# Mask maxima split on GpSimd, a shorter log series and a scalar head-norm shift, with all orders laid anew, in a fused attention and Mamba2 kernel

## The chip, the cores and the metric

One core of one Trainium2 chip runs the kernel. The metric is the device time of one execution in microseconds (us), given as the median of several runs. PE is TensorE, DVE is VectorE, ACT is ScalarE, POOL is GpSimd, and SP is SyncE, which here only issues transfers.

## What is computed

64 sequences of 128 tokens with 256 features pass a cross-attention layer with a layer norm, a Mamba2 block and a second cross-attention. Cut to what matters:

```python
q = relu(queries @ Wq + bq); k = relu(keys @ Wk + bk); v = relu(values @ Wv + bv)   # 16 heads of 16
scores = where(row_mask, q_ @ k_ / sqrt(16), 1e-9)
x = layernorm(softmax(scores) @ v_ + queries) * gamma + beta
zxbcdt = rms(x, norm_w) @ in_proj_w                       # z 512, xBC 768, dt 8
dt = softplus(zxbcdt[..., -8:] + dt_bias)
xBC = silu(conv4(xBC) + conv_b)
h = h * exp(dt * A) + (dt * xh) B ; y = h C               # scan over the tokens, state 128
x = x + rms((y + D_skip * xh) * silu(z), gnorm_w) @ out_proj_w
out = x + softmax(ln(x) @ Wq (enc @ Wk)^T / sqrt(32)) @ (enc @ Wv) @ Wo    # 8 heads of 32
```

## The kernel before, in words

Sequences go in 32 groups `g` of two sequences `b` (NB = 2), each with 256 tokens. Every engine has one program: small functions (pieces) such as `q(g, m)` or `scan(g, b)`, and behind them a list of calls that is written out by hand. The list has a head, a loop `for g in range(NG - 9)` of 23 turns, in which pieces of up to six groups interleave (`k(g+7, 0)` of a late group beside `wp(g+2, 0)` of an early one), and a tail. Each engine works through its list in order; semaphores tie the engines together. A wait stands inside the piece that needs it. A turn of the loop is one group's worth of work.

Matrix products go to eight PSUM banks. The table `USES` says which bank each of the 63 uses of a turn takes; `bank()` (line 183) looks up the use before it in the same bank and returns the semaphore that tells it is free. So a new order needs a new table. `unread()` and `warm()` are matmuls whose results nobody reads; they fill places in head and tail.

The pieces the change and the prediction speak of:

- **q, k, v, sA** (PE). Projections as three products of high and low halves (line 332), and the raw scores, for their maxima (line 399). ACT splits the inputs, `split_x` (line 1384) and `split_c` (1395), and evicts, `qe` (1416), `ke` (1427, two or four pieces) and `ve` (1439). POOL forms the low halves, `lo_x` (1842) and `lo_c` (1847), and multiplies the row mask in, `qm` (1861).
- **mA, nm, nw** (DVE). `mA` (line 835) takes the negated maxima of 16 heads, 128x16 numbers for a sequence. `nm` (line 847) casts them to the matmul's type into `NM`, `nw` (line 854) writes the remainder. TensorE transposes `NM` in `tn` (line 412), ACT writes `NT` (line 1449), and the second scores `sT` (lines 432 and 436) use it to subtract the maxima. `eA` (1463) takes the exponential; `av` (456) and `ot` (442) follow, then on DVE `rc` (863), the reciprocal of the sum, `xo`, and the layer norm.
- **cp, dp, bd** (PE). In-projection, the dt columns and a transpose. DVE does the convolution's `tap` (line 991) and `xc` (1004), ACT `ac` and `th`.
- **dc** (DVE, line 940 on). Softplus needs log(1 + u). With r = u / (u + 2) it is 2 r (1 + r^2/3 + r^4/5 + ...) to r^12/13, written as 12 steps on 128x16 numbers; each waits for the one before.
- **scan, lg, yd** (DVE, lines 1015, 1024, 1044). The decay goes out to DRAM and comes back spread over 128 partitions as `DB`, 512 KB for a sequence.
- **hs, hg, hr, hm** . Norm of the second attention. `hm` (DVE, line 1081) computes minus mean times the reciprocal deviation, one number a partition, for ACT's `hx`. `r2` (POOL, 1952) is the power of the RMS norm.
- **tC, sC, oC, q1, k1, v1, wp** (PE). Second attention. `fin` and `store` end a group.

SP issues all loads and stores: `load_x` (line 236, tile xT), `load_c` (243, cT), `load_t` (258, xt), `load_u` (267, cT again for the second attention), `load_m` (280, QM, 128 KB), `dec_out` (286), `dec_in` (294, DB) and `store` (300). All but QM, DB and `dec_out` are 256 KB. A load waits until the tile's last reader is done, and what is behind it waits as well.

Of the kernel before, what the change touches and what calls it, by code (L numbers as in the profile page):

```python
# [2116 lines left out]
```

## Time and profile before

| what | before |
| --- | --- |
| three runs | 1319.29, 1319.77, 1320.99 us, median 1319.77 |
| the profiled execution | span 1319.5 us (its own time is not given beside it) |
| PE busy | 1303.4 us, 99% |
| DVE busy | 1193.6 us, 90% |
| ACT busy | 1131.2 us, 86% |
| POOL busy | 947.7 us, 72% |
| DMA | 87.03 MB, mean 66 GB/s |

The span is from the first to the last instruction of the profiled execution. Busy time is the time in which an engine executed at least one instruction; for PE the ends of matmuls are modelled. The DMA queue q1 carries the kernel's own transfers, q8 and q14 carry instructions to the engines. A share of busy time is a mean over head, loop and tail, which differ.

### The profile page before, as it was taken

The page shows a single profiled execution, that of the slowest core. Times are in us where ns is not written, and L with a number is a line of the kernel's source. Part 1 is how long each engine was busy: PE and PEld are TensorE (multiplying, and loading weights), DVE is VectorE, ACT ScalarE, POOL GpSimd, SP SyncE. Part 2 cuts the span into 40 slices and gives each one's busy share as a digit, 9 for nine tenths or more (in the row PEclk, how much of TensorE's full clock was granted, in tenths as well). Part 3 has the DMA queues.
Part 4 walks back from the last instruction along what each step waited for, and adds up shares of the span by engine and source line. Part 5 has one row for each costly group of instructions (what it writes and reads, how often), then busy time and mean ns, then how long its engine had stood idle before and what let it go on. Part 6 is the DMA issues. An engine that isn't in the chain of part 4 may idle for free.

```text
span 1319.5 us, 43916 instructions
## 1 busy us (share of the span) xinstructions
PE 1303.4 (99%) x15877; PEld 1165.5 (88%) x15877; DVE 1193.6 (90%) x3032; ACT 1131.2 (86%) x3407; POOL 947.7 (72%) x1214
## 2 busy tenths in 40 slices
PE   8999999999999999999999999999999999999998
PEld 7888888999888898888998888899888889898887
DVE  6999999999999999999999999999999999999882
ACT  6778888898888898888898888899888899888866
POOL 4777777777777777777677777687777677677674
PEclk9999999999999999999999999999999999999999
DMA  6121122212122212122211122211122222011210
GB/s 208 48 74 50 50 74 78 78 49 67 50 70 78 78 50 66 50 70 78 78 57 59 50 70 78 78 60 57 50 70 78 77 82 62 17 51 58 66 49 25
DMA packets 41285, 87.03 MB, mean 66 GB/s; under 512 B 5744, under 2 KB 10992, under 8 KB 41072
## 3 DMA queue, kind: packets, MB, share of 16 engines
q1 hardware_dynamic: 40560, 83.93, 20.4%
q8 instruction: 129, 2.11, 0.7%
q14 instruction: 84, 0.69, 0.2%
q10 hardware_dynamic: 512, 0.31, 0.1%
HBM read 75.53 MB, written 8.68 MB: 64 GB/s over the span
## 4 chain that ended last, share of the span: by engine, by line
PE 92%; DVE 4%; POOL 2%; issue 1%; DMA 1%; ACT 1%; DVEq 0%; ACTq 0%; POOLq 0%
PE bank L332 28%; PE bank L442 11%; PE bank L573 7%; PE bank L432 5%; PE bank L399 5%; PE bank L456 5%; PE bank L556 5%; PE bank L587 4%; PE bank L692 4%; PE bank L627 3%; PE bank L380 3%; PE bank L648 3%; PE bank L677 2%; PE bank L490 2%; PE bank L436 1%; PE bank L531 1%
## 5 line engine op out<-in xcount | busy, mean ns | idle before, releaser
L991 DVE SCALAR_TENSOR_TENSOR ACC<-bank,cw,ACC 128x250 f32<-128x250 f32 (+2 forms) x576 | 264.5, 462 | 6.4 <-ACT ACC L1561 3.7
L332 PE MATMUL bank<-xnT,wnl 128*128 128x256 f32 x640 | 198.6, 310 | 1.7 <-DVE XC L1004 1.4
L1648 ACT ACTIVATE PC<-bank,stc 128x128 f32<-128x128 f32 x512 | 182.8, 388 | 8.0 <-DVE stc L1103 5.2
L332 PE MATMUL bank<-xnL,wnh 128*128 128x256 f32 x640 | 178.7, 279 | 0.0
L332 PE MATMUL bank<-xnT,wnh 128*128 128x256 f32 x640 | 178.3, 279 | 0.0
L835 DVE TENSOR_REDUCE sta<-bank 128x4 f32<-128x512 f32 x256 | 163.6, 672 | 2.8 <-PE bank L399 2.8
L1015 DVE TENSOR_TENSOR_SCAN L<-DB,id 128x1024 f32<-128x1024 f32 x64 | 146.6, 2290 | 2.2 <-DMA DB<-dec_scratch 2.2
L1967 POOL TENSOR_TENSOR PC<-PC,stc 128x512 f32<-128x512 f32 x128 | 132.4, 1043 | 11.7 <-DVE stc L1110 11.5
L1463 ACT ACTIVATE PTA<-bank 128x512 f32<-128x512 f32 x256 | 133.5, 629 | 6.8 <-PE bank L436 3.9
L332 PEld LDWEIGHTS bank<-xnT,wnl 128*128 128x128 f32 x640 | 120.4, 188 | 21.4 <-issue 16.2
L1922 POOL TENSOR_TENSOR XH<-XH,dtt 128x512 f32<-128x512 f32 x64 | 81.0, 1265 | 56.6 <-ACT XH L1578 56.6
L332 PEld LDWEIGHTS bank<-xnL,wnh 128*128 128x128 f32 x640 | 120.8, 189 | 0.1
L332 PEld LDWEIGHTS bank<-xnT,wnh 128*128 128x128 f32 x640 | 120.1, 188 | 0.0
L1648 ACT ACTIVATION_READ_ACCUMULATOR PC<-bank,stc 128x1 f32 x512 | 116.7, 228 | 0.0
L1847 POOL TENSOR_TENSOR cL<-cT,cH 128x512 fp32r<-128x512 f32 x31 | 59.0, 1903 | 76.8 <-ACT cH L1395 76.8
L1561 ACT ACTIVATE ACC<-bank,cw 128x256 f32<-128x256 f32 x192 | 110.6, 577 | 2.2 <-PE bank L332 1.5
L1931 POOL TENSOR_TENSOR Y<-Y,SZ 128x512 f32<-128x512 f32 x64 | 85.9, 1342 | 18.8 <-DVE Y L1044 16.1
L1937 POOL TENSOR_TENSOR Yl<-Y,Yh 128x512 fp32r<-128x512 f32 x64 | 82.2, 1285 | 17.4 <-ACT Yh L1606 17.4
L1449 ACT ACTIVATE NT<-bank,sel 128x128 fp32r<-128x128 f32 x256 | 73.6, 382 | 21.5 <-PE bank L412 21.5
L1662 ACT ACTIVATE PTC<-bank 128x512 f32<-128x512 f32 x128 | 78.8, 622 | 15.3 <-PE bank L442 15.2
L1103 DVE TENSOR_REDUCE stc<-bank 128x4 f32<-128x512 f32 x128 | 84.3, 681 | 6.9 <-PE bank L652 6.7
L1569 ACT ACTIVATE bank<-ACC 128x256 f32<-128x256 f32 x192 | 79.6, 418 | 11.1 <-DVE ACC L991 10.8
(210 smaller groups left out, 4757.7 us busy)
## 6 DMA issues: line engine op xcount, KB each, us to landing
DB<-dec_scratch SPq DMA_DIRECT2D x64, 512.0 KB, 4.0
cT<-in_cT SPq DMA_DIRECT2D x64, 256.0 KB, 2.7
xt<-in_xt SPq DMA_DIRECT2D x32, 256.0 KB, 3.7
out_x<-X SPq DMA_DIRECT2D x32, 256.0 KB, 4.0
xT<-in_xT SPq DMA_DIRECT2D x31, 256.0 KB, 4.1
QM<-qm_rows SPq DMA_DIRECT2D x31, 128.0 KB, 4.0
XC<-in_win SPq DMA_DIRECT2D x2, 644.0 KB, 6.8
PTC<-in_wout SPq DMA_DIRECT2D x2, 256.0 KB, 4.6
```

The costliest lines, as they stand in the source:

```text
L332: mm = e.matmul(t[:, c0:c0 + T], wt[:, k, m:m + 128], x[:, k, :], start=(n == 0), stop=(n == 5))
L442: mm = e.transpose(t[:, c0 + i * 128:c0 + (i + 1) * 128], src(i), ident[:, :])
L573: e.matmul(t[:, 0:256], x[:, kk * 128:(kk + 1) * 128], w[:, kk, :], start=(n == 0), stop=(n == 11))
L835: e.tensor_reduce(sta[ns % 4][:, 4 * j:4 * j + 4], t[:, :].rearrange("p (i k) -> p i k", i=4), AX_X, ALU.max, negate=True).then_inc(s_mA, 1)
L991: e.scalar_tensor_tensor(out=w, in0=t[:, 0:T].rearrange("p (b t) -> p b t", b=NB)[:, :, 0:125 + k], scalar=cw[:, c, k:k + 1], in1=w, op0=A ...
L1015: e.tensor_tensor_scan(L[:, :, :].rearrange("p h t -> p (h t)"), DB[b][:, :], id8[:, :, :].rearrange("p h t -> p (h t)"), 0.0, ALU.mult, A ...
L1103: e.tensor_reduce(stc[g % 4][:, 4 * i:4 * i + 4], t[:, :].rearrange("p (i k) -> p i k", i=4), AX_X, ALU.max, negate=True).then_inc(s_mC, 1)
L1463: e.activation(PTA[n % 4][:, :, :], t[:, :].rearrange("p (i k) -> p i k", i=4), ACT.Exp).then_inc(s_eA, 1)
L1561: e.activation(ACC[n % 3][:, :, :], t[:, 0:T].rearrange("p (b t) -> p b t", b=NB), ACT.Identity, bias=cw[:, c, 4:5], scale=cw[:, c, 3:4]). ...
L1648: op = e.activation(PC[n % 4][:, p, :], t[:, p * 128:(p + 1) * 128], ACT.Exp, bias=stc[g % 4][:, 4 * i + p:4 * i + p + 1], accum_out=stc[g ...
L1931: e.tensor_tensor(cv(Y[:, :]), cv(Y[:, :]), SZ[:, :, b * 128:(b + 1) * 128], ALU.mult).then_inc(s_ga, 1)
L1967: e.tensor_tensor(PC[n % 4][:, :, :], PC[n % 4][:, :, :], stc[g % 4][:, 16 + 4 * i:20 + 4 * i].unsqueeze(2).to_broadcast([128, 4, 128]), A ...
```

## The change

1. `nm` and `nw` leave DVE's program and stand in POOL's (lines 1861 and 1868 of the changed kernel), with the same waits.
2. The log series has five fitted coefficients for its seven terms, so `dc` has 10 steps and not 12.
3. `hm` is a `tensor_scalar` with the second factor as a per-partition scalar.
4. SP waits for `d_qr` ahead of the second group of late weights, and DVE's first `xs` for the small parameters.
5. The orders of all five engines and the bank table are new. Each turn has the same 55 pieces on PE, 68 on ACT and 9 on SP; DVE has 88 for 94, POOL 33 for 29. The dummy matmuls keep their counts; only their places shift.

```diff
+ATANH = (1.000000004, 0.33333157341, 0.20012455137, 0.13980301434, 0.14089167199)
 USES = [
-    (("k", 1, 1), 3), (("ot", 0, 2), 5), (("z", 1, 3), 2), (("sT", 4, 2), 1), (("sT", 5, 2), 5), (("sT", 6, 2), 6),
+    (("k", 1, 1), 3), (("ot", 0, 2), 0), (("z", 1, 3), 2), (("sT", 4, 2), 5), (("sT", 5, 2), 0), (("sT", 6, 2), 1),
...
                     if g == 2:
+                        e.wait_ge(d_qr, 16)
...
         def vector(e):
...
-            def nm(g, b):
-                if ok(g):
-                    ns = 2 * g + b
-                    w = sta[ns % 4][:, 0:16].rearrange("p (j i) -> p j i", j=4)
-                    if ns == 0:
-                        e.wait_ge(z_pad, 9)
-                    if ns >= 2:
-                        e.wait_ge(s_tn, ns - 1)
-                    e.wait_ge(s_mA, 4 * ns + 4)
-                    e.tensor_copy(NM[ns % 2][:, :, 0:4], w).then_inc(s_nm, 1)
-
-            def nw(g, b):
...
-                    e.wait_ge(s_nm, ns + 1)
-                    e.tensor_tensor(NM[ns % 2][:, :, 4:8], w, NM[ns % 2][:, :, 0:4].bitcast(F32), ALU.subtract).then_inc(s_nw, 1)
...
+                    if ns == 0:
+                        e.wait_ge(d_small, 16 * 4)
                     e.wait_ge(s_bg, ns + 1)
...
-                        op = e.tensor_scalar(f, d[4], 1 / 13, None, ALU.mult)
-                    elif i < 9:
-                        op = e.scalar_tensor_tensor(out=f, in0=f, scalar=1 / (19 - 2 * i), in1=d[4], op0=ALU.add, op1=ALU.mult)
-                    elif i == 9:
-                        op = e.scalar_tensor_tensor(out=f, in0=f, scalar=1.0, in1=d[3], op0=ALU.add, op1=ALU.mult)
-                    elif i == 10:
+                        op = e.tensor_scalar(f, d[4], ATANH[4], None, ALU.mult)
+                    elif i < 7:
+                        op = e.scalar_tensor_tensor(out=f, in0=f, scalar=ATANH[7 - i], in1=d[4], op0=ALU.add, op1=ALU.mult)
+                    elif i == 7:
+                        op = e.scalar_tensor_tensor(out=f, in0=f, scalar=ATANH[0], in1=d[3], op0=ALU.add, op1=ALU.mult)
+                    elif i == 8:
...
-                    e.scalar_tensor_tensor(out=w[:, 10:11], in0=w[:, 2:3], scalar=-1.0, in1=w[:, 3:4],
-                                           op0=ALU.mult, op1=ALU.mult).then_inc(s_hm, 1)
+                    e.tensor_scalar(w[:, 10:11], w[:, 2:3], w[:, 3:4], -1.0, ALU.mult, ALU.mult).then_inc(s_hm, 1)
...
             for g in range(NG - 9):
+                dec_out(g + 3)
+                load_m(g + 6)
                 load_c(g + 6)
-                dec_out(g + 3)
                 dec_in(g + 3, 0)
-                load_m(g + 6)
+                store(g)
+                dec_in(g + 3, 1)
                 load_x(g + 7)
                 load_u(g + 3)
-                dec_in(g + 3, 1)
                 load_t(g + 5)
-                store(g)
...
         def gpsimd(e):
...
+            def nm(g, b):
...
+                    e.tensor_copy(NM[ns % 2][:, :, 0:4], w).then_inc(s_nm, 1)
+
+            def nw(g, b):
...
```

**The head of ACT.** In the program's first pieces ACT had four KT pieces and then the split of the second x (tile xH); below first the order before, then that of the change.

```order
L1416 ACTIVATE QT<-bank,pc 128x256 x2
L1427 ACTIVATE KT<-bank,kb,par 128x2x128 x4
L1384 ACTIVATE xH<-xT 128x512
L1439 ACTIVATE V<-bank 128x32x16
L1395 ACTIVATE cH<-cT 128x512
```

```order
L1384 ACTIVATE QT<-bank,pc 128x256 x2
L1352 ACTIVATE xH<-xT 128x512
L1395 ACTIVATE KT<-bank,kb,par 128x2x128 x4
L1407 ACTIVATE V<-bank 128x32x16
L1384 ACTIVATE QT<-bank,pc 128x256
```

The split of x, which waits for a transfer, has moved from behind the four KT pieces to before them, and V stays behind both. On POOL `lo_x(1)` moved in the same way between the two `qm`, and on PE the first half of `q(1, ...)` moved ahead of the first `sA`.

**POOL in the loop.** The tiles are `stb` (head norm and RMS), `QT`, `xL` (low half of x) and, for the split, `NM` and `sta`. First a stretch of the turn before, then of the change.

```order
L1943 TENSOR_TENSOR SQ<-SQ 128x256
L1945 TENSOR_TENSOR SQ<-SQ 128x128
L1967 TENSOR_TENSOR PC<-PC,stc 128x512
L1852 TENSOR_TENSOR cUl<-cT,cUh 128x512
L1861 TENSOR_TENSOR QT<-QT,QM 128x256
L1952 TENSOR_TENSOR stb<-stb,mhalf 128x1
L1861 TENSOR_TENSOR QT<-QT,QM 128x256
```

```order
L1949 TENSOR_TENSOR PC<-PC,stc 128x512 x2
L1806 TENSOR_TENSOR xL<-xT,xH 128x512
L1934 TENSOR_TENSOR stb<-stb,mhalf 128x1
L1868 TENSOR_TENSOR NM<-sta,NM 128x4x4
L1825 TENSOR_TENSOR QT<-QT,QM 128x256
L1816 TENSOR_TENSOR cUl<-cT,cUh 128x512
```

The subtraction `nw` of the second sequence stands behind `xL` and the power of the RMS norm; its cast `nm` stands some ten rows further ahead. The transpose on PE that waits for it, `tn(g + 6, 1)`, moved from behind the four `av` pieces to right behind `bd`.

**SP in the tail.** These are the transfers around the last group's decay but one (`dec_scratch` is the decay's way out, `DB` its way in), before and changed.

```order
L286 DMA dec_scratch<-decT 16x128
L300 DMA out_x<-X 128x512
L258 DMA xt<-in_xt 128x512
L267 DMA cT<-in_cT 128x512
L294 DMA DB<-dec_scratch 128x1024 x2
L300 DMA out_x<-X 128x512
```

```order
L260 DMA xt<-in_xt 128x512
L288 DMA dec_scratch<-decT 16x128
L296 DMA DB<-dec_scratch 128x1024
L302 DMA out_x<-X 128x512 x2
L296 DMA DB<-dec_scratch 128x1024
L269 DMA cT<-in_cT 128x512
```

The load of xt has moved ahead of the decay, and cT behind both DB transfers, with two stores between these.

## Rows read from the trace of the kernel before

**Rows 1.** Page: busy time of each engine; the chain that ended last
```profile
PE 1303.4 (99%) x15877; PEld 1165.5 (88%) x15877; DVE 1193.6 (90%) x3032; ACT 1131.2 (86%) x3407; POOL 947.7 (72%) x1214
...
PE 92%; DVE 4%; POOL 2%; issue 1%; DMA 1%; ACT 1%; DVEq 0%; ACTq 0%; POOLq 0%
```

**Rows 2.** Busy us by stretch: PE, PEld, DVE, ACT, POOL; clock, DMA share, GB/s
```profile
0.00:20.00 20.00, 16.72 (x160) 15.42 (x161) 11.35 (x23) 10.35 (x21) 8.13 (x25) 1.00 0.80 250
...
592.29:631.80 39.51, 39.51 (x489) 35.42 (x489) 36.82 (x95) 34.95 (x107) 28.89 (x37) 1.00 0.23 65
...
1290.00:1319.50 29.50, 24.31 (x236) 20.27 (x235) 7.88 (x23) 17.65 (x67) 11.63 (x16) 1.00 0.08 28
```

**Rows 3.** Waits of TensorE, whole span: waiter, releaser, us, times, longest
```profile
PE bank L332 <- issue: 2.2, 1, 2.2
PE bank L332 <- DVE XC L1004: 1.4, 3, 0.6
...
PE bank L692 <- ACT OT L1672: 1.3, 2, 0.9
```

**Rows 4.** Groups of VectorE in 592.29 to 631.80: count, busy us, mean ns
```profile
L1081 DVE SCALAR_TENSOR_TENSOR stb<-stb 128x1 f32<-128x1 f32 x2 | 1.2, 605 | 0.0
...
L963 DVE SCALAR_TENSOR_TENSOR bank<-bank,dts 128x16 f32<-128x16 f32 x5 | 0.9, 172 | 0.0
...
L847 DVE CAST NM<-sta 128x16 fp32r<-128x16 f32 x2 | 0.3, 165 | 0.0
```

**Rows 5.** Timeline of VectorE, POOL and TensorE: start, us, line, operation
```profile
599.42 0.72 DVE L1081 SCALAR_TENSOR_TENSOR stb<-stb 128x1 f32<-128x1 f32 x1
...
598.83 1.29 POOL L1842 TENSOR_TENSOR xL<-xT,xH 128x512 fp32r<-128x512 f32 x1
...
600.36 0.33 PE L412 MATMUL bank<-ident,NM 128*128 128x128 f32 x1
```

**Rows 6.** Groups of POOL in 592.29 to 631.80
```profile
L1961 POOL TENSOR_TENSOR stb<-stb,mhalf 128x1 f32<-128x1 f32 x2 | 1.1, 564 | 0.2
...
L1893 POOL TENSOR_SCALAR sta<-sta 128x1 f32<-128x1 f32 x2 | 0.4, 218 | 0.2 <-DVE sta L891 0.2
```

**Rows 7.** Timeline of ACT, 7 to 26 us
```profile
9.18 1.93 ACT L1427 ACTIVATE KT<-bank,kb,par 128x256 f32<-128x256 f32 x4 [0.47 <-PE bank L332]
13.08 0.63 ACT L1384 ACTIVATE xH<-xT 128x512 fp32r<-128x512 f32 x1 [1.97 <-DMA xT<-in_xT]
13.62 0.58 ACT L1439 ACTIVATE V<-bank 128x512 f32<-128x512 f32 x1
```

**Rows 8.** Timeline of TensorE, 9 to 27 us
```profile
14.25 1.15 PE L399 MATMUL bank<-KT,QT 32*128 32x256 f32 x16 [1.32 <-ACT V L1439]
...
21.30 1.12 PE L432 MATMUL bank<-QT,KT 32*128 32x128 f32 x29 [0.45 <-ACT KT L1427]
```

**Rows 9.** Waits of TensorE, 20 to 80 us
```profile
PE bank L332 <- DVE XC L1004: 0.8, 2, 0.5
...
PE bank L490 <- DVE xnL L923: 0.5, 1, 0.5
```

**Rows 10.** Timeline of VectorE and of TensorE, 1228 to 1250 us
```profile
1238.91 2.29 DVE L1015 TENSOR_TENSOR_SCAN L<-DB,id 128x1024 f32<-128x1024 f32 x1 [2.18 <-DMA DB<-dec_scratch]
...
1242.43 0.28 PE L332 MATMUL bank<-cUh,wk1h 128*128 128x256 f32 x1 [2.23 <-issue]
```

**Rows 11.** DMA, 1230 to 1239.9: packets, MB, share; issues, KB, us to landing
```profile
q1 hardware_dynamic: 890, 2.10, 65.3%
...
DB<-dec_scratch SPq DMA_DIRECT2D x2, 512.0 KB, 8.1
```

**Rows 12.** DMA queues, 1239.9 to 1241
```profile
q8 instruction: 1, 0.02, 5.5%
```

**Rows 13.** DMA, 592.29 to 631.80
```profile
q8 instruction: 4, 0.07, 0.7%
...
DB<-dec_scratch SPq DMA_DIRECT2D x2, 512.0 KB, 3.7
```

More of the change, by code:

```diff
@@ L776, in tensor @@
                 bd(g + 5, 0)
+                tn(g + 6, 1)
                 cp(g + 5, 5)
@@ new lines, in vector @@
+            tap(0, 12); tap(0, 13); tap(0, 14); xc(0, 3); rc(1, 0); tap(0, 15); xo(1, 0); tap(0, 16); tap(0, 17)
+            bs(1, 0); bg(1, 0); xc(0, 4); xs(1, 0); xc(0, 5); sz(0, 1); x2(1, 0); scan(0, 0); mA(2, 0); rc(1, 1)
+            mA(2, 1); xo(1, 1); mA(2, 2); mA(2, 3); bs(1, 1); bg(1, 1); lg(0, 0); xs(1, 1); x2(1, 1); mA(2, 4)
+            yd(0, 0); mA(2, 5); scan(0, 1); nl(1, 0); nl(1, 1); mA(2, 6); lg(0, 1); mA(2, 7); d0(1, 0); tap(1, 0)
+            d0(1, 1); yd(0, 1); dc(1, 0); tap(1, 1); dc(1, 1); tap(1, 2); dc(1, 2); tap(1, 3); dc(1, 3); tap(1, 4)
@@ new lines, in vector @@
+            xc(1, 0); dc(1, 4); dc(1, 5); tap(1, 5); dc(1, 6); r1(0, 0); dc(1, 7); xc(1, 1); tap(1, 6); dc(1, 8)
+            sz(1, 0); tap(1, 7); hh(0, 0); tap(1, 8); dc(1, 9); r1(0, 1); hs(0, 0); hh(0, 1); xc(1, 2); tap(1, 9)
+            tap(1, 10); dk(1, 0); hs(0, 1); hg(0, 0); tap(1, 11); tap(1, 12); tap(1, 13); xc(1, 3); tap(1, 14)
+            tap(1, 15); rc(2, 0); tap(1, 16); xo(2, 0); tap(1, 17); hg(0, 1); xc(1, 4); bs(2, 0); bg(2, 0); xc(1, 5)
+            hm(0, 0); sz(1, 1); kk1(0, 0); xs(2, 0); hm(0, 1); x2(2, 0); kk1(0, 1); scan(1, 0); mA(3, 0); rc(2, 1)
@@ new lines, in vector @@
+            xo(2, 1); mA(3, 1); mA(3, 2); bs(2, 1); bg(2, 1); lg(1, 0); xs(2, 1); mA(3, 3); x2(2, 1); mA(3, 4)
+            mA(3, 5); yd(1, 0); mA(3, 6); mA(3, 7); scan(1, 1); nl(2, 0); nl(2, 1); mC(0, 0); mC(0, 1); d0(2, 0)
+            d0(2, 1); lg(1, 1); mC(0, 2); tap(2, 0); dc(2, 0); dc(2, 1); dc(2, 2); yd(1, 1); dc(2, 3); mC(0, 3)
+            tap(2, 1); dc(2, 4); rC(0, 0); dc(2, 5); dc(2, 6); dc(2, 7); tap(2, 2); xc(2, 0); r1(1, 0); dc(2, 8)
+            tap(2, 3); rC(0, 1); tap(2, 4); tap(2, 5); tap(2, 6); dc(2, 9); xc(2, 1); sz(2, 0); r1(1, 1); hh(1, 0)
@@ new lines, in vector @@
+            tap(3, 12); hg(2, 1); xc(3, 3); tap(3, 13); hm(2, 0); tap(3, 14); tap(3, 15); rc(4, 0); xo(4, 0)
+            tap(3, 16); tap(3, 17); bs(4, 0); bg(4, 0); xc(3, 4); xc(3, 5); xs(4, 0); sz(3, 1); rC(1, 3); kk1(2, 0)
+            hm(2, 1); x2(4, 0); scan(3, 0); mA(5, 0); kk1(2, 1); rc(4, 1); xo(4, 1); mA(5, 1); mA(5, 2); bs(4, 1)
+            mA(5, 3); bg(4, 1); lg(3, 0); xs(4, 1); mA(5, 4); x2(4, 1); mA(5, 5); yd(3, 0); mA(5, 6); mA(5, 7)
+            scan(3, 1); nl(4, 0); nl(4, 1); mC(2, 0); lg(3, 1); d0(4, 0); mC(2, 1); d0(4, 1); mC(2, 2); tap(4, 0)
@@ L1224, in vector @@
+            xc(4, 4); bs(5, 0); hm(3, 0); bg(5, 0); xc(4, 5); sz(4, 1); hm(3, 1); xs(5, 0); kk1(3, 0); x2(5, 0)
+            scan(4, 0); mA(6, 0); kk1(3, 1); rc(5, 1); xo(5, 1); rC(2, 3); mA(6, 1); mA(6, 2); bs(5, 1); mA(6, 3)
+            bg(5, 1); lg(4, 0); mA(6, 4); xs(5, 1); x2(5, 1); mA(6, 5); yd(4, 0); mA(6, 6); mA(6, 7); scan(4, 1)
+            nl(5, 0); nl(5, 1); mC(3, 0); lg(4, 1); mC(3, 1); d0(5, 0); tap(5, 0); d0(5, 1); mC(3, 2); rC(3, 0)
             for g in range(NG - 9):
+                yd(g + 4, 1)
+                mC(g + 3, 3)
@@ new lines, in vector @@
+            tap(NG - 4, 8); hh(NG - 5, 1); tap(NG - 4, 9); rC(NG - 6, 1); xc(NG - 4, 2); tap(NG - 4, 10)
+            dk(NG - 4, 0); hm(NG - 5, 0); tap(NG - 4, 11); hs(NG - 5, 1); rC(NG - 6, 2); hg(NG - 5, 1); rC(NG - 6, 3)
+            tap(NG - 4, 12); tap(NG - 4, 13); xc(NG - 4, 3); tap(NG - 4, 14); rc(NG - 3, 0); tap(NG - 4, 15)
+            xo(NG - 3, 0); xc(NG - 4, 4); tap(NG - 4, 16); tap(NG - 4, 17); sz(NG - 4, 1); xc(NG - 4, 5)
+            bs(NG - 3, 0); hm(NG - 5, 1); kk1(NG - 5, 0); scan(NG - 4, 0); mA(NG - 2, 0); mA(NG - 2, 1); mA(NG - 2, 2)
@@ new lines, in vector @@
+            tap(NG - 3, 13); tap(NG - 3, 14); xc(NG - 3, 3); rC(NG - 5, 3); hm(NG - 4, 0); tap(NG - 3, 15)
+            rc(NG - 2, 0); xc(NG - 3, 4); xo(NG - 2, 0); tap(NG - 3, 16); tap(NG - 3, 17); bs(NG - 2, 0)
+            bg(NG - 2, 0); sz(NG - 3, 1); xc(NG - 3, 5); hm(NG - 4, 1); xs(NG - 2, 0); kk1(NG - 4, 0); x2(NG - 2, 0)
+            scan(NG - 3, 0); mA(NG - 1, 0); rc(NG - 2, 1); mA(NG - 1, 1); xo(NG - 2, 1); mA(NG - 1, 2); mA(NG - 1, 3)
+            bs(NG - 2, 1); bg(NG - 2, 1); xs(NG - 2, 1); lg(NG - 3, 0); kk1(NG - 4, 1); x2(NG - 2, 1); mA(NG - 1, 4)
@@ new lines, in vector @@
+            tap(NG - 1, 14); xc(NG - 1, 3); rC(NG - 3, 3); tap(NG - 1, 15); hs(NG - 2, 1); tap(NG - 1, 16)
+            xc(NG - 1, 4); tap(NG - 1, 17); hg(NG - 2, 1); fin(NG - 4, 0); xc(NG - 1, 5); hm(NG - 2, 1)
+            scan(NG - 1, 0); lg(NG - 1, 0); kk1(NG - 2, 0); sz(NG - 1, 1); kk1(NG - 2, 1); yd(NG - 1, 0)
+            scan(NG - 1, 1); mC(NG - 2, 0); lg(NG - 1, 1); rC(NG - 2, 0); yd(NG - 1, 1); mC(NG - 2, 1); r1(NG - 1, 0)
+            mC(NG - 2, 2); hh(NG - 1, 0); hs(NG - 1, 0); rC(NG - 2, 1); mC(NG - 2, 3); hg(NG - 1, 0); fin(NG - 3, 0)
@@ L1715, in scalar @@
                 hx(g + 2, 1)
-                n1(g + 4, 0)
                 he(g + 2, 0)
```

692 lines of the change are left out of this document (324 added, 368 removed), and 16 rows, old and new, of the table USES.

## The prediction

> **What bounds the kernel now.** I read the page first. TensorE is busy for 1303.4 of 1319.5 us and carries 92% of the chain that ended last, VectorE 4% [rows 1]. So at most some 16 us could ever come back unless TensorE is given less to do. The table of stretches says where they are [rows 2]: TensorE misses 3.28 us in the first 20, nothing in a turn of the loop (39.51 of 39.51 us, with VectorE at 36.82), 5.19 us in the last 29.5, of which the closing work after the last matmul is a part. The granted clock is 1.00 in each, so the clock enters nowhere. The waits of TensorE name what is behind the gaps [rows 3]: the largest is 2.2 us in which it waited for nothing that the profile shows, then come 1.4 us for VectorE's XC and 1.3 for ACT's OT.
>
> The change leaves TensorE's work as it is: each turn has the same 55 pieces, the dummy matmuls keep their counts. TensorE has no gap in a turn [rows 2], so a piece costs the same wherever it stands in the queue as long as what it reads is there; I cost the reordering of the turn at nothing. Every gain or loss must therefore come from gaps, unless the change opens new ones.
>
> **The change part by part, in a turn of the loop.** The split of the maxima leaves VectorE: two casts and two subtractions, at the cast's duration 4 x 0.165 = 0.66 us, about 0.5 in time, since starts lie closer than durations [rows 4]. The log series loses two of its short steps, 2 x 0.17 = 0.34 recorded, about 0.2 in time. The head-norm shift (hm) is the dearest of the small ones: 0.605 us for one element per partition. The timeline tells why [rows 5]: hm starts at 599.42 and ends at 600.14, and the POOL operation beside it runs from 598.83 to 600.12; hm ends when that one ends. It reads two operands from SBUF; its new form names the second as a per-partition scalar. If that ends the blocking, it falls to the 0.165 of its neighbours [rows 4], 2 x 0.44 = 0.9 us; if not, 0. Together VectorE gets back 0.7 to 1.6 us a turn, from 36.82 busy. TensorE waits for it nowhere there, so in the loop this is worth **0**, and the cover is TensorE's own full queue.
>
> POOL takes the split. Its nearest rows are 0.218 us for a one-element TENSOR_SCALAR and 0.564 us for a one-element TENSOR_TENSOR that holds a power [rows 6]; the cast and the subtraction of 16 elements lie between, nearer the lower, 4 x 0.25 = 1 us a turn (0.9 to 2.3). POOL is busy 28.89 of 39.51 [rows 2], so it has room. What counts is who waits: the transpose tn of group g+6 follows nm and nw, and the second tn moves forward, ahead of cp 5 and the four av pieces. It ran at 600.36 [rows 5], and some 1.8 us of matmuls that stood ahead of it now stand behind it, so it comes near 598.6. On POOL nw stands behind xL (1.29) and the RMS power (0.56); with the order known and 10.6 us idle a turn I put its end near 597.6. The slack is about 1 us, and I cost this at **0** too, with the other end for the rivals.
>
> **The head.** Here a move costs. ACT did four KT pieces from 9.18 to 11.11 and then idled 1.97 us until xT(1) had landed; xH ran at 13.08 and V at 13.62, ending at 14.20 [rows 7]. TensorE's first sA waited 1.32 us for that V and began at 14.25 [rows 8]. In the new order xH, which waits for the load, stands ahead of the KT pieces: behind xH come 1.93 us of KT and 0.58 of V, so that V ends at about 13.6 + 1.93 + 0.58 = 16.1. The load itself cannot come earlier, being the first on its queue before and after. The first sA moves from 14.25 to about 16.15, **+1.9 us**. q(1,0), now ahead of it, fills part of the gap, but from there a chain of latencies runs through the maxima, their split, tn, NT and KT to the first sT at 21.30 [rows 8], with TensorE filled up by 14 dummies, and moves as a whole. The split on POOL adds some 0.2 to it at 0.25 each against 0.17; this I keep for the range.
>
> What of it is regained? From 20 to 80 us TensorE waits 0.8 us for XC and 0.5 for xnL [rows 9], 1.3 us in all, behind that first chain. When TensorE is late these waits shrink, and VectorE, which they wait for, is about 0.6 us a turn lighter (split and series). Its own chain moves with sA too, however. Between 0 and 1.3, and some smaller ones beside these, I take **-0.8**. Head: **+1.1** (+0.4 to +2.1).
>
> **The tail.** The wait of 2.23 us for nothing visible lies at 1240.2 to 1242.43 [rows 10]. In the 9.9 us before it queue q1 moved 2.10 MB at 65.3% of all engines [rows 11], and no instruction packets went; right after, in 1239.9 to 1241, one packet on q8 did [rows 12]. A turn has four such fetches [rows 13]. I read the wait as TensorE's instructions having been kept out by the burst of loads. Two DB transfers took 8.1 us in it [rows 11] against 3.7 in the loop [rows 13], and VectorE's scan waited 2.18 us for one of them [rows 10]. The new order puts xt ahead of the decay's way out, takes cT behind both DBs, and sends the first DB ahead of all others: the scan's wait mostly goes. 1.8 MB remain in one piece (two DBs, two outputs, cT), starting some 1.1 us later. Scaled from 2.10 MB in 9.9 us that is 8.5 us, so it ends at about 1239.6 and not 1239.9, if it isn't torn apart; if it is (its second DB waits for a buffer that the scan frees), the fetch slips in early. I take half the stall away, -1.1, between none and all. Half of that I count as lost again, since TensorE next meets VectorE's chain, whose steps don't get shorter by it. That gives -0.55 (0 to -2.2). The pieces behind (three taps fewer ahead of the last groups' heads, the last tC ahead of the dummies) are worth another -0.35 (+0.3 to -1.0), an estimate from TensorE's 5.19 us of idle in the last stretch [rows 2] and its 1.3 us of waits for OT [rows 3], both in that stretch. Tail: **-0.9** (+0.3 to -3.2).
>
> The Trainium skill (Runtime: NRT & Kernel Launch, section Instruction fetch mechanics) says that the next page of 16 KiB is fetched while the current one runs, and that the crossing is mostly hidden. By that rule the 2.23 us would have another cause and would stay, and the sum would be 0.55 higher. The trace speaks against the rule here: the one packet on q8 comes directly before TensorE goes on.
>
> **Sum.** 1319.5 + 1.1 + 0 - 0.9 = **1319.7 us**. The profiled execution's span is 1319.5, the median of the three runs 1319.77, so the two bases differ by 0.3 at most.
>
> **The rivals.**
> *Faster.* The burst no longer holds the fetch up, and the stall goes as a whole (-2.2); the last stretch gives -1.0; the head regains all but 0.4: 1319.5 - 2.2 - 1.0 + 0.4 = **1316.7**, down to 1315.5 if most of the 1.4 us behind XC [rows 3] goes too. For it: three separate short waits named in the rows, a lighter VectorE. Against: the tail is a chain of latencies in which one removed wait hands over to the next.
>
> *Slower, by starved fetches in the loop.* The loop's loads went in two parts, one DB in each, and so each DB took only 3.7 us [rows 13]. Now QM, cT, DB, out, DB and xT stand one behind the other: 128 + 256 + 512 + 256 + 512 + 256 KB = 1.9 MB, nearly the tail's 2.10 [rows 11]. At that burst's rate it takes 9.0 us. TensorE comes to a new page of instructions every 39.51 / 4 = 9.9 us [rows 13], and the tail's burst of 9.9 us made a fetch too late; so from about 9.9 us on, contention of the other queues counted in, each turn pays. At 0.3 us a turn over 23 turns that is +6.9, **1326.6**; at the tail's whole 2.2 it would be +50. Against it: the waits inside the SP queue (DB waits for the decay's way out, each load for its buffer) tear the burst apart, and the other fetches of a turn lie outside it.
>
> *Slower, by POOL.* If cast and subtraction take 0.56 each, and the power ahead of nw waits longer for VectorE, nw ends after 598.6 and TensorE waits at tn in each turn: 0.2 us x 23 = +4.6, **1324.3**.
>
> *Loss kept.* The head regains nothing (+2.1) and the stall stays: 1319.5 + 2.1 - 0.35 = **1321.3**. For it: the new ACT order is certain, the regaining is not.
>
> *The change does less than it says.* hm may stay as slow as it is, as POOL's operation still runs beside it; then VectorE's share falls by 0.7 and not by 1.6, with no change in the time, for TensorE doesn't wait for it.
>
> **How the numbers follow.** A measurement of this kernel can tell some 0.2% from no change, 2.6 us: below 1317.1 is faster, above 1322.4 slower. Chances: the forecast 0.47, loss kept 0.14 (both within), faster 0.24, starved fetches 0.10, POOL 0.05. So faster 0.24, same 0.61, slower 0.15. The range goes from the faster case's lower end, 1315.5, to 1323.0, the forecast's upper ends (+2.1 and +0.3, with the POOL term and the run's 1 us of scatter); the two slower cases are what it leaves out, 0.15.
>
> **What would show it.** Right: the first sA at about 16.1 and the first sT near 23.2; turns of 39.5 us as before with VectorE at 35 to 36; the two hm at about 0.17; POOL near 29.9 a turn; in the tail a stall of TensorE's issue of about 1 us and a scan that waits under 1. Wrong: turns longer than 39.6 us with waits for "issue" (fetches) or at tn; a head whose waits for XC and xnL vanish or don't move at all; a tail stall of 0 or over 2.

## The result, and the profile after

The changed kernel took 1334.22 us (median of 4 runs, 1332.85 to 1335.83) against 1319.59: ratio 1.0103, 95% interval 1.0085 to 1.0122. It is 14.6 us slower by the medians, 13.6 by the ratio. The forecast was 1319.7, its range ended at 1323.0. The profiled execution has a span of 1331.5 us and a time of its own of 1333.25; in it and in all the executions profiled since, own time and span lie 1.75 to 1.87 us apart.

The waits of TensorE over the whole span answer to [rows 3]:

```profile
PE bank L458 <- ACT PTA L1431: 4.1, 1, 4.1
PE bank L533 <- DVE sta L837: 2.2, 1, 2.2
PE bank L334 <- POOL xL L1806: 2.0, 1, 2.0
```

None of these three rows stands in that view of the kernel before. The table of stretches, with columns as in [rows 2], shows where they lie and what came with them:

```profile
30.00:35.00 5.00, 3.28 (x51) 2.66 (x49) 4.71 (x10) 0.51 (x2) 3.84 (x5) 1.00 0.97 329
35.00:40.00 5.00, 2.47 (x34) 1.38 (x35) 0.00 (x0) 4.25 (x9) 0.97 (x1) 0.73 0.04 11
40.00:45.00 5.00, 4.88 (x52) 3.95 (x50) 3.06 (x8) 4.14 (x10) 2.38 (x4) 0.93 0.00 0
640.95:680.31 39.36, 39.36 (x491) 35.42 (x490) 35.84 (x89) 34.80 (x107) 31.63 (x42) 1.00 0.21 66
1194.00:1236.15 42.15, 39.09 (x468) 34.06 (x467) 36.70 (x90) 31.72 (x99) 28.38 (x38) 0.96 0.15 45
```

The wait of 4.1 us runs from 33.4 to 37.5. Behind it the granted clock is 0.73 and then 0.93 of full speed, so that for part of that time TensorE ran at 1.2 and not at 2.4 GHz; the same comes, weaker, behind the wait of 2.2 us at 1214 and one of 0.68 us that follows it (0.83 from 1215 to 1225). A turn of the loop is shorter than before, 39.36 us against 39.51, and so in most turns. Cut at the wp pieces, the span divides so: up to the second one, 207.14 us against 197.06 (+10.1); 22 turns from there, 866.9 against 869.1 (-2.3); the rest 257.5 against 253.3 (+4.2). Together +12.0, the difference of the two spans. One trace of a head can be some 3 us off: in e13 below, whose head is that of the kernel before, the second wp came at 200.53 us, in e6, e9 and e17 at 197.2 to 197.4.

The 4.1 us has a chain behind it. The waits of ACT in the changed kernel, 28 to 38 us:

```profile
ACT wk1h L1429 <- DMA wo<-in_wo: 5.2, 1, 5.2
```

SP's issues, its timeline from 15 us on (start, us, line):

```profile
15.00 0.33 SPq L237 DMA_DIRECT2D xT<-in_xT  x1
15.38 0.91 SPq L282 DMA_DIRECT2D QM<-qm_rows  x2
26.38 0.33 SPq L237 DMA_DIRECT2D xT<-in_xT  x1
26.75 1.28 SPq L244 DMA_DIRECT2D cT<-in_cT  x1
...
30.46 0.43 SPq L254 DMA_DIRECT2D wo<-in_wo  x1
```

And POOL's timeline in the same stretch, with the idle time ahead of an instruction in brackets:

```profile
23.46 0.38 POOL L1861 CAST NM<-sta 128x16 fp32r<-128x16 f32 x1 [3.13 <-DVE sta L837]
23.93 0.47 POOL L1868 TENSOR_TENSOR NM<-sta,NM 128x16 fp32r<-128x16 f32 x1
...
25.05 1.30 POOL L1806 TENSOR_TENSOR xL<-xT,xH 128x512 fp32r<-128x512 f32 x1
```

Read from below: on POOL the split (CAST and TENSOR_TENSOR on NM) of the second sequence's maxima waits 3.13 us for VectorE, and xL(2) stands behind it. SP's load_x(3) waits for xL(2) from 16.3 to 26.4. In the new order load_c(2), and with it six loads of late weights, stands behind load_x(3). ACT needs the weights at 30.5 and has them at 35.75. ACT's PTA for the second sequence stands behind them, and TensorE waits for PTA. Before, load_c(2) was issued at 16.3 and wo at 19.4.

### The profile page after: what moved, and what is told of

Same layout as the page of the kernel before. It is cut to its first block, busy times and chain, and to the rows that moved or that the text cites. A ratio compares the mean times of both kernels' runs of the same rounds, so it can differ in the third digit from the quotient of the medians.

```text
span 1331.5 us, 43853 instructions
## 1 busy us (share of the span) xinstructions
PE 1306.5 (98%) x15877; PEld 1167.7 (88%) x15877; DVE 1166.1 (88%) x2840; ACT 1128.2 (85%) x3407; POOL 1018.2 (76%) x1342
## 3 DMA queue, kind: packets, MB, share of 16 engines
q1 hardware_dynamic: 40560, 83.93, 19.4%
## 4 chain that ended last, share of the span: by engine, by line
PE 91%; DVE 3%; DMA 2%; POOL 2%; issue 1%; ACT 1%; SPq 0%; ACTq 0%; DVEq 0%; POOLq 0%
PE bank L334 27%; PE bank L444 11%; PE bank L575 7%; PE bank L401 5%; PE bank L434 5%; PE bank L558 5%; PE bank L458 5%; PE bank L694 4%; PE bank L589 4%; PE bank L629 3%; PE bank L382 3%; PE bank L650 3%; PE bank L679 2%; PE bank L492 2%; PE bank L438 1%
## 5 line engine op out<-in xcount | busy, mean ns | idle before, releaser
L977 DVE SCALAR_TENSOR_TENSOR ACC<-bank,cw,ACC 128x250 f32<-128x250 f32 (+2 forms) x576 | 267.7, 470 | 30.7 <-ACT ACC L1529 27.6
L334 PE MATMUL bank<-xnT,wnl 128*128 128x256 f32 x640 | 201.8, 315 | 2.1 <-DVE XC L990 1.1
L837 DVE TENSOR_REDUCE sta<-bank 128x4 f32<-128x512 f32 x256 | 166.5, 674 | 13.1 <-PE bank L401 13.1
L1001 DVE TENSOR_TENSOR_SCAN L<-DB,id 128x1024 f32<-128x1024 f32 x64 | 157.9, 2467 | 1.3 <-DMA DB<-dec_scratch 1.3
L1949 POOL TENSOR_TENSOR PC<-PC,stc 128x512 f32<-128x512 f32 x128 | 133.3, 1042 | 13.6 <-DVE stc L1095 13.5
L1904 POOL TENSOR_TENSOR XH<-XH,dtt 128x512 f32<-128x512 f32 x64 | 87.1, 1360 | 42.8 <-ACT XH L1546 42.8
L1616 ACT ACTIVATION_READ_ACCUMULATOR PC<-bank,stc 128x1 f32 x512 | 112.3, 219 | 0.0
L1811 POOL TENSOR_TENSOR cL<-cT,cH 128x512 fp32r<-128x512 f32 x31 | 78.9, 2545 | 40.0 <-ACT cH L1363 40.0
L1850 POOL TENSOR_TENSOR xa<-xa,xt 128x256 f32<-128x256 f32 x64 | 47.5, 742 | 69.0 <-DVE xa L857 68.9
```

Source lines behind the costliest of these rows:

```text
L334: mm = e.matmul(t[:, c0:c0 + T], wt[:, k, m:m + 128], x[:, k, :], start=(n == 0), stop=(n == 5))
L837: e.tensor_reduce(sta[ns % 4][:, 4 * j:4 * j + 4], t[:, :].rearrange("p (i k) -> p i k", i=4), AX_X, ALU.max, negate=True).then_inc(s_mA, 1)
L977: e.scalar_tensor_tensor(out=w, in0=t[:, 0:T].rearrange("p (b t) -> p b t", b=NB)[:, :, 0:125 + k], scalar=cw[:, c, k:k + 1], in1=w, op0=A ...
L1001: e.tensor_tensor_scan(L[:, :, :].rearrange("p h t -> p (h t)"), DB[b][:, :], id8[:, :, :].rearrange("p h t -> p (h t)"), 0.0, ALU.mult, A ...
L1616: op = e.activation(PC[n % 4][:, p, :], t[:, p * 128:(p + 1) * 128], ACT.Exp, bias=stc[g % 4][:, 4 * i + p:4 * i + p + 1], accum_out=stc[g ...
L1904: e.tensor_tensor(hv(XH[:, :]), hv(XH[:, :]), dtt[g % 3][:, b * 8:b * 8 + 8].unsqueeze(2).to_broadcast([128, 8, 64]), ALU.mult).then_inc(s ...
```

## The experiments

Each run was timed in five rounds beside the kernel before on the same chip. Ratios are to that kernel. Gains in us between two runs are differences of their medians; the kernel before itself came out at 1319.0 to 1320.0 in these sessions, so they can be off by about 1 us, and where that matters the gain by the ratios is given too.

**The late weights and one store.** Four runs:

```diff
# e1_weights_first, changed kernel, SP's head
-load_m(2); load_x(3); load_c(2); load_m(3)
+load_m(2); load_c(2); load_x(3); load_m(3)
# e2_before_weights_late, kernel before, SP's head
-load_m(2); load_c(2); load_c(3); load_m(3); load_x(3);
+load_m(2); load_x(3); load_c(2); load_c(3); load_m(3);
# e3_store_first, changed kernel, SP's tail (e4_both: e1 and e3)
-load_t(NG - 2); dec_out(NG - 3); load_u(NG - 3); dec_in(NG - 3, 0); dec_in(NG - 3, 1); store(NG - 7)
+load_t(NG - 2); store(NG - 7); dec_out(NG - 3); load_u(NG - 3); dec_in(NG - 3, 0); dec_in(NG - 3, 1)
```

> The changed kernel with one call moved in SP's head: load_c(2), with the late weights behind it, stands ahead of load_x(3) again. Theory 1 (the late weights are what costs the head: load_x(3) waits for xL(2) until 26.4 us, wo lands at 35.7 instead of about 24, TensorE waits 4.1 us and its clock falls to 0.73 in 35 to 40): the gap at 33.4 goes, the clock stays at 1.00 in 30 to 45, and the time falls by 6 to 9 us to 1325 to 1328. Rival 1 (the head's loss comes from the new order of ACT and POOL, the weights are only late beside it): the gap comes back behind another wait, and the time falls by under 2 us.

1329.96 us, ratio 1.0076 (1.0061 to 1.0091): 4.3 us faster than the changed kernel (3.6 by the ratios), between theory and rival. The wait of 4.1 us is gone and the clock is 1.00 in 30 to 45, as theory 1 said. Up to the second wp it took 202.43 us, and so 4.7 less. Some 5 us of the head stay.

> The kernel before with load_x(3) put ahead of load_c(2) in SP's head, nothing else. xL(2) is written at 23.3 us there, so the weights are issued from about 23.4 and wo lands near 32, against a first use at 28.5. Theory 1: slower by 3 to 6 us, with a wait of ACT for wo of 3 us and a gap of TensorE of 2 to 3 us near 30. Rival 1: within 1.5 us of the kernel before.

1323.25 us against 1319.03, 1.0027 (1.0018 to 1.0036), +4.2: as theory 1. ACT waited 3.2 us for wo, TensorE 3.4 for PTA. The same swap takes from the one kernel what it gives to the other.

> The changed kernel with store(NG - 7) put ahead of dec_out(NG - 3) in SP's tail. There VectorE waited 1.5 us for that store before it could write X, its scan ended at 1213.85, TensorE waited 2.17 us, and the clock was 0.96 in 1194 to 1236. Theory 2 (the place of this store costs the tail): 2 to 4 us faster than the changed kernel, about 1331. Rival 2 (the turns before it are late for other reasons, 40.1 and 40.2 us, and the wait only moves): under 1 us.

1330.75 us, 1.0083 (1.0065 to 1.0100): 3.5 us faster (2.6 by the ratios), theory 2. In the changed kernel, 1205 to 1216, VectorE's row was

```profile
DVE X L895 <- DMA out_x<-X: 1.5, 1, 1.5
```

X2 is a ring of five, so group NG - 2 writes where NG - 7 stood, and its store had moved behind two DB transfers. With the store ahead of them TensorE's wait of 2.2 us and the clock of 0.96 are gone; 1194 to 1236 has 1.00.

> Both moves of the two runs before in the changed kernel. If head and tail are independent the gains add: 1334.2 - 7.5 - 3 = about 1323.5 (1321 to 1326), some 4 us above the kernel before, of which 1.9 is the first sA.

1324.93 us, 1.0040 (1.0026 to 1.0054): 9.3 us faster (8.3 by the ratios), inside the expectation. Two places in SP's queue are some three fifths of the loss.

**Is it the maxima on POOL?** In the changed kernel only POOL's head was touched, SP's order left as it is:

```diff
# e11_xL_ahead_of_maxima
-nw(0, 0); nm(0, 1); nw(0, 1); qm(1, 0); lo_x(2); qm(1, 1)
+nw(0, 0); lo_x(2); nm(0, 1); nw(0, 1); qm(1, 0); qm(1, 1)
```

> The changed kernel with one call moved on POOL's head: lo_x(2) ahead of nm(0, 1), SP as the change has it. Theory 7 (the split of the maxima on POOL is why the late weights came so late: xL(2) stood behind nm(0, 1), which waits for VectorE's maxima until 23.4 us, and load_x(3) and all weights behind it wait for xL(2)): xL(2) is written at about 21.5 and not 26.4, the weights are issued 4 to 5 us earlier, the gap of 4.1 us shrinks to under 0.5, the clock stays at 1.00, and the time falls by 4 to 7 us. Rival 7 (SP's order alone decides): under 1.5 us.

1330.66 us, 1.0080 (1.0065 to 1.0094), 3.6 us faster (3.0 by the ratios), a little under the span expected but well over the rival's. load_x(3) is issued at 21.80, wo at 25.0, and the wait of 4.1 us is under 0.2. So the loss needs both: the split ahead of xL(2) on POOL, and load_x(3) ahead of the weights on SP. Either one undone, it goes.

**What is left of the head.** On top of e4_both:

```diff
# e5_head_order: ACT, POOL and TensorE
-qe(0, 1); split_x(1); ke(0, 0); ke(0, 1); ve(0, 0)
+qe(0, 1); ke(0, 0); ke(0, 1); split_x(1); ve(0, 0)
-qm(0, 0); lo_x(1); qm(0, 1)
+qm(0, 0); qm(0, 1); lo_x(1)
-v(0, 0); q(1, 0); sA(0, 0); q(1, 1)
+v(0, 0); sA(0, 0); q(1, 0); q(1, 1)
# e14_xL_ahead_in_e5: e5 with POOL's lo_x(2) as in e11
# e16_first_split_on_vector: e5 with nm and nw of (0, 0) and (0, 1) on VectorE behind mA(0, 3) and mA(0, 7)
```

> The run with both moves (e4_both), and the head of three queues as before: ACT does the four KT pieces ahead of the split of x(1), POOL both mask products ahead of xL(1), TensorE the first sA ahead of q(1,0). Theory 3 (my +1.9 for the first sA): the first sA comes 1.5 to 2 us earlier and the time falls by 1.3 to 2 us, to about 1323.2. Rival 3 (TensorE's later waits in the head, 0.65 for XC, 0.67 for QT, are of other chains and take it up): under 0.7 us.

1323.88 us, 1.0030 (1.0019 to 1.0042). By the ratios that is 1.3 us faster than e4_both, by the distance to the kernel before 1.7: the size of theory 3, though the two intervals overlap. The trace of e5 is of its slowest execution, and its first sA stands at 15.94 us, not earlier. In e14 and e16 below, with the same order there, it stands at 14.51 and 14.36, against 15.67 in e4_both.

> The run e5_head_order with lo_x(2) ahead of nm(0, 1) on POOL as in e11. What is left above the kernel before there is 4.2 us. Theory 9 (the rest of the head is latency that starts with the blocked xL(2), since q(2, 0) stands ahead of the second sT in TensorE's new order): 1 to 2.5 us faster than e5. Rival 9 (the new order of TensorE's head in itself): within 0.5 us of e5.

> The run e5_head_order with nm and nw of the first two sequences back on VectorE, behind their maxima, the rest on POOL. Theory 9: as e14 or better, since xL(2) is free and the first split takes 0.4 us and not 0.7: 1.2 to 3 us faster than e5. Rival 9: within 0.7 us of e5.

1323.71 us, 1.0026 (1.0016 to 1.0035), and 1323.02, 1.0024 (1.0014 to 1.0033): 0.5 and 0.8 us by the ratios, neither apart from e5. Theory 9 isn't borne out at its size. Some 3.3 us stay, although the turns give 2.3 back, so the new orders of head and tail still cost between 5 and 6. The traces divide it, cut as above. In the head, e10, e14 and e16 reach the second wp at 200.8 to 201.2 us, the kernel before, e6, e9 and e17 at 197.1 to 197.4. Behind the 22 turns, e3, e4, e5, e10, e14 and e16 take 253.5 to 254.4 us, those with the old tail (e2, e6, e9, e17) 250.8 to 252.1. So some 3.5 lie in the head and 2 to 3 in the tail. Which pieces carry them is open; e16's head shows no wait over 0.7 us that the old one hasn't too.

**Why is a turn shorter?** I first suspected the places of the transposes.

```diff
# e6_tn_ahead_of_av, kernel before: tn(g + 6, 1) ahead of av(g + 6, 0..3)
# e7_both_tn: that, and
-z(g + 5, 0); v1(g + 3, 0); cp(g + 5, 2); wp(g + 2, 0); tn(g + 6, 0)
+v1(g + 3, 0); z(g + 5, 0); tn(g + 6, 0); cp(g + 5, 2); wp(g + 2, 0)
# e10_tn_behind_wp, on e5: cp(g + 5, 2); wp(g + 2, 0); tn(g + 6, 0)
```

> The kernel before with one call moved in TensorE's loop: tn(g + 6, 1) ahead of the four av pieces instead of behind them. A turn took 39.36 us in the changed kernel and 39.51 before, with no gap in either; the pieces whose duration changed are the tn, av and wo ones. Theory 4 (the transpose costs at its edges, between tiled pieces more than between full-array ones): some 0.05 to 0.1 us a turn less, 1.2 to 2.5 us in all. Rival 4 (a turn's gain has nothing to do with tn): no change.

1319.70 against 1319.72 us, 1.0004 (0.9995 to 1.0013), a turn 39.50: no change.

> The kernel before with both transposes at the places where the change has them or near them: tn(g + 6, 1) ahead of av, and v1, z, tn(g + 6, 0), cp 2, wp in that order. Theory 4: 0.15 us a turn less, 3.4 us in all, about 1315.9. Rival 4: no change, or slower where v1, now ahead of z, waits for its bank.

1354.98 us, 1.0268 (1.0251 to 1.0285), 35 us slower. The row of TensorE's waits says why:

```profile
PE bank L412 <- ACT V L1638: 29.8, 23, 2.4
```

tn and v1 share bank 0. With z alone between them tn waits each turn until ACT has evicted v1, whose place in ACT's order I had not moved. One row of one engine moved by two places cost more than the whole change.

> The run e5_head_order with tn(g + 6, 0) put back behind cp 2 and wp in TensorE's loop, where the kernel before has it. Theory 4 (what is left of it: not the second transpose, which made no difference in e6, but the first, which stood between wp and cp 3): a turn takes 39.50 us and not 39.36, the time rises by 2.5 to 3.5 us to about 1327. Rival 4: no change.

1323.80 us, 1.0030 (1.0018 to 1.0041), a turn 39.37. Theory 4 has fallen for both transposes.

**The edits without the orders.** The next four put them into the kernel before one by one.

```diff
# e17_hm_alone
-e.scalar_tensor_tensor(out=w[:, 10:11], in0=w[:, 2:3], scalar=-1.0, in1=w[:, 3:4], op0=ALU.mult, op1=ALU.mult)
+e.tensor_scalar(w[:, 10:11], w[:, 2:3], w[:, 3:4], -1.0, ALU.mult, ALU.mult)
# e8_series_and_hm_in_place: that and the series in 10 steps; calls dc(g, 10) and dc(g, 11) do nothing
# e9_waiting_step_kept: the same, but calls dc(g, 4) and dc(g, 5) do nothing
# e15_split_on_pool_in_loop: e9, and in POOL's loop
 dx(g + 3, 1)
+nm(g + 5, 1)
...
 r2(g + 3, 1)
+nw(g + 5, 1)
...
 xd(g + 4, 0)
+nm(g + 6, 0)
 xr(g + 5, 1)
+nw(g + 6, 0)
```

> The kernel before with two of the three edits in place and no order changed: the log series in 10 steps and the head-norm shift as a tensor_scalar; the split of the maxima stays on VectorE. By the prediction VectorE gets up to 1.1 us a turn back and the time stays within 1 us (1318.5 to 1320). Rival 5 (a lighter VectorE starts transfers earlier or closes waits in head and tail): 1 to 2 us faster.

1349.96 us, 1.0225 (1.0211 to 1.0239). A shorter series, 30 us slower. VectorE in one turn, 640 to 680 us:

```profile
DVE dts L971 <- ACT dtt L1545: 2.6, 1, 2.6
```

Before it was 0.4 us. The last step of the series multiplies by what ACT makes of the step before. With the last two calls left empty it had slid two calls forward in VectorE's queue, and all that stands behind it waited with it.

> As e8 (series in 10 steps and hm as a tensor_scalar in the kernel before), but the two steps that are left out are calls 4 and 5, so that the last step, which waits for ACT's dtt, stays where it stood, two calls later than in e8. Theory 6 (e8 lost 30 us because that step came earlier in VectorE's queue, waited 2.6 us a turn for ACT and held back what stood behind it): the wait is again 0.4 us, a turn takes 39.5 us, the time is 1317.5 to 1320.5. Rival 6 (a lighter VectorE or the new hm form disturbs the turn in itself): a turn stays over 40 us, the time over 1340.

1318.13 us, 0.9991 (0.9983 to 1.0000). The wait is 0.4 us again, a turn 39.39 (39.5 was expected): theory 6.

> The kernel before with the tensor_scalar form of hm alone. hm took 0.605 us in a turn; in the changed kernel 0.206. Theory 11 (the wait of 0.11 us a turn of TensorE's weight load for ACT's PTA goes with VectorE's 0.8 us): a turn takes 39.39 us, 1.5 to 3 us faster in all. Rival 11 (it was the shorter series, which is on dt's way to ACT): a turn stays at 39.50.

1317.51 us against 1319.76, **0.9981 (0.9972 to 0.9990)**: the best of all, faster than both kernels. hm takes 0.200 us. A turn takes 39.39 us, so the new form of hm alone shortens it by 0.12; the series adds nothing that these runs can tell. Where TensorE gains is a row of its weight loads, over the whole span. The kernel before:

```profile
PEld bank L456 <- ACT PTA L1463: 6.6, 33, 0.3
```

And e17, as a row of the same view:

```profile
PEld bank L456 <- ACT PTA L1462: 1.9, 8, 0.3
```

In nearly every turn the weight load of av waited up to 0.3 us for ACT's exponential. Piece by piece the two turns of before and e9 differ in one place: from av to sA, 0.11 us.

The way from hm to av can be followed in the timelines of VectorE, POOL and ACT in one turn. The kernel before:

```profile
638.94 0.70 DVE L1081 SCALAR_TENSOR_TENSOR stb<-stb 128x1 f32<-128x1 f32 x1
638.33 1.29 POOL L1842 TENSOR_TENSOR xL<-xT,xH 128x512 fp32r<-128x512 f32 x1
640.06 0.39 ACT L1569 ACTIVATE bank<-ACC 128x256 f32<-128x256 f32 x1 [0.23 <-DVE ACC L991]
```

The same turn of e17, which began 0.76 us earlier:

```profile
638.17 0.19 DVE L1081 TENSOR_SCALAR stb<-stb 128x1 f32<-128x1 f32 x1
637.57 1.30 POOL L1841 TENSOR_TENSOR xL<-xT,xH 128x512 fp32r<-128x512 f32 x1
638.93 0.42 ACT L1568 ACTIVATE bank<-ACC 128x256 f32<-128x256 f32 x1
```

Behind hm stands a tap of the convolution (ACC), and ACT's tanh waits for that tap. With hm 0.51 us shorter the tap ends 0.51 earlier, ACT no longer waits, and it is 0.30 us ahead until its next exponential, which begins 0.15 earlier in the turn. The 32 matmuls of that av then take 1.08 us and not 1.19.

> The kernel before with all three edits and no new orders: e9 with nm and nw of the 46 sequences from (5, 1) to (28, 0) on POOL, at the places the change has them in the loop (behind dx, r2, xd and xr), the others still on VectorE; each nm and nw also waits for the one before it. A turn took 39.39 us in e9. By my slack of 1 us and more for tn: no wait at tn, VectorE 0.5 us lighter, a turn within 0.03 us of 39.39, time within 1 us of e9. Rival 10 (POOL's later pieces are what the turn waits for): a turn over 39.5 us, slower by 3 us or more.

1332.30 us, 1.0087 (1.0073 to 1.0101), a turn 39.81: rival 10, 14 us slower than e9 (12.7 by the ratios). POOL's timeline of that run, 619.5 to 624 us:

```profile
620.59 0.20 POOL L1904 CAST NM<-sta 128x16 fp32r<-128x16 f32 x1 [1.30 <-DVE sta L836]
620.74 0.73 POOL L1891 TENSOR_TENSOR xa<-xa,xt 128x256 f32<-128x256 f32 x1
```

VectorE's in the same stretch:

```profile
621.50 0.43 DVE L890 BATCH_NORM_STATS2 sta<-xa 128x6 f32<-128x256 f32 x1 [1.08 <-POOL xa L1891]
```

The cast waits 1.30 us for the maxima, with xr (tile xa) behind it. VectorE waits 1.08 us for xa, its product L (1.20 us from 622.07) ends later, and TensorE's y stands 0.36 us each turn. The tn that I had looked at had over a microsecond of slack. In the changed kernel xr stands ahead of that cast, and the turn is short.

**The tail's loads.**

```diff
# e13_before_new_tail_loads, kernel before
-dec_out(NG - 2); store(NG - 6); load_t(NG - 1); load_u(NG - 2); dec_in(NG - 2, 0); dec_in(NG - 2, 1); store(NG - 5)
+load_t(NG - 1); dec_out(NG - 2); dec_in(NG - 2, 0); store(NG - 6); store(NG - 5); dec_in(NG - 2, 1); load_u(NG - 2)
```

> The kernel before with the change's order of SP's calls around the last group's decay but one: load_t(NG - 1), dec_out(NG - 2), dec_in 0, store, store, dec_in 1, load_u. In the changed kernel the stretch from the sixth last wp to the next took 43.1 us against 45.6, and TensorE's issue wait of 2.23 us was gone. Theory 8 (the burst kept TensorE's instructions out, and the order of loads decides): the issue wait falls under 0.5 us and VectorE's scan waits under 1 us for DB; 1.5 to 2.5 us faster than before, about 1317.4. Rival 8 (half is handed on to the next wait): 0.5 to 1.2 us faster.

1319.71 against 1320.02 us, 0.9996 (0.9987 to 1.0005). The issue wait is gone, and VectorE's scan no longer waits for a DB, but the time hardly moves. The reason is in the other traces: e2, e6, e7, e8, e9, e15 and e17 keep the old tail order, and none of them has that issue wait, while their scan waited for a DB, 0.4 to 1.4 us at a time against 2.2. The issue wait came in one traced execution of eight, and the medians show no cost of it. What caused it no run shows.

## Why the prediction was wrong, by its steps

The step that failed is the path through SP's queue. The sum had no term for a load or a store that the new orders hold back: the head was put at +1.1 and came out at +10.1 in the traces, the tail at -0.9 and came out at +4.2, or at +5.4 to +6.7 against the traces of the old tail that have no issue wait (e2, e6, e9, e17).

- **The base.** I set the span of 1319.5 beside the median of 1319.77 as if alike. With the 1.75 to 1.87 us between own time and span of the later executions, that execution took about 1321.3 (an estimate), 1.7 over the median of 1319.59. It carried the issue wait of 2.23 us that no other trace of that tail shows. The tail's -0.55 had nothing to stand on.
- **The first sA.** Right: 16.15 and 23.2 expected, 16.00 and 23.18 in the profile. e5 gives it back at 1.3 to 1.7 us.
- **"What of it is regained", -0.8.** Here the head failed. I looked for waits that would shrink, and not for what the later xL(2) would delay. The sentence "The load itself cannot come earlier, being the first on its queue" was true of xT(1) and passed over the next waiting load. My sum took account neither of POOL's split standing ahead of xL(2) nor of load_x(3) standing ahead of load_c(2). That is 4 to 6 us with the clock behind it: 4.3 in e1, 4.2 in e2, and 5.8 between e3 and e4. The waits that were to shrink are no gain either: from 20 to 80 us TensorE still waits 0.8 us for XC, the 0.5 for xnL is gone, and waits of 0.7 each for NM and QT are new. What e4_both leaves is 5.3 us over the kernel before by the ratio, and with the 2.3 us that the turns give back 7.6, the cost of the new orders in head and tail. Of that, e5 and e16 took back some 2.
- **The store in the tail.** No term at all for store(NG - 7) behind the DBs: +3.5 (2.6 by the ratios).
- **A turn, "worth 0".** Wrong: it was -0.14 us in most turns, -2.3 over the 22 that I cut out. "TensorE has no gap in a turn" was read from busy time, whose ends are modelled; the weight loads' waits showed 0.2 us a turn. In the old order the new hm alone gives 0.12 of the 0.14; that it is the same in the new order is argued, not shown, though there too nearly all of these waits are gone (6 in e10, 33 before).
- **VectorE's and POOL's costs.** Right. hm 0.605 to 0.208, VectorE 35.84 busy (35 to 36 expected), cast 0.201 and subtraction 0.222, and nw of the second sequence ends 1.1 us ahead of its tn in turn after turn. POOL's total, 31.63, is 1.7 over what I gave. Of that 1.05 is cL, 2.97 us instead of 1.92: it now starts 0.4 us behind the start of VectorE's scan of 2.28 us, and started 1.5 us behind it before.
- **Rivals.** Starved fetches: no, no turn shows the wait. POOL ahead of tn: no, though e15 shows POOL's split costing 13 to 14 us through another reader. No rival had a load held back in SP's queue.
- **Not settled.** Which pieces in the new orders carry the last 5 to 6 us, some 3.5 in the head and 2 to 3 in the tail, of which the turns give 2.3 back.

The group of hm on VectorE in a turn of the changed kernel, 640.95 to 680.31, which answers to [rows 4]:

```profile
L1067 DVE TENSOR_SCALAR stb<-stb 128x1 f32<-128x1 f32 x2 | 0.4, 208 | 0.2 <-POOL stb L1943 0.2
```

And POOL's groups in the same turn, to [rows 6]:

```profile
L1811 POOL TENSOR_TENSOR cL<-cT,cH 128x512 fp32r<-128x512 f32 x1 | 3.0, 2973 | 1.2 <-ACT cH L1363 1.2
...
L1868 POOL TENSOR_TENSOR NM<-sta,NM 128x16 fp32r<-128x16 f32 x2 | 0.4, 222 | 0.0
...
L1861 POOL CAST NM<-sta 128x16 fp32r<-128x16 f32 x2 | 0.4, 201 | 0.0
```

## What to carry to other kernels

When an operation that waits moves to another queue, or a waiting step moves forward in its own, its own duration and its direct reader are the small part; list what stands behind it, and follow each of those to the loads they release. In an order written by hand, removing an operation moves every wait behind it: 2 of 12 steps left out at the wrong place cost 30 us, at the right place nothing. A new form of one instruction, put in alone with the order kept, was worth more than the whole new order.

## What the runs showed of the hardware

- A VectorE instruction on one element per partition with two SBUF operands took 0.605 us on average in a turn. Beside POOL's xL it took 0.70 to 0.72 and ended when xL ended; the few times nothing ran beside it on POOL, 0.14 to 0.22. With the second operand as a per-partition scalar it took 0.200, and 0.19 beside the same xL. The Trainium skill (SBUF — State Buffer, Who interferes with whom) says that a VectorE instruction with two SBUF inputs contends with a GpSimd instruction that reads SBUF, and that one with at most one SBUF input, outside the two-port modes, does not. The traces agree, with the scalar operand not acting as a second input.
- TensorE's clock fell after a wait of 4.1 us (0.73 and 0.93 from 35 to 45 us) and after one of 2.2 us that a wait of 0.68 followed (0.83 from 1215 to 1225 us, 0.96 over 42 us). Where e1 and e3 removed the wait, the clock there was 1.00. A wait of 2.2 us alone did not always do it: behind the kernel before's of 2.23 us at 1242 the clock stayed at 1.00.
- An issue wait of 2.23 us, which I had read as one for instructions, came in one of the eight executions traced with that order of loads. The Trainium skill (Runtime: NRT & Kernel Launch, Instruction fetch mechanics) calls the cost of crossing to the next page of instructions mostly hidden. The other seven traces agree with it, and I had taken the one that seemed against it for the rule.
